# Attention on one Trainium2 core: text queries packed into five tiles per unit, and the turned image probabilities of three heads copied by ScalarE

## The reference, cut to what matters

```
h    = concat(mixer(x), txt)                       # 16 x (128 + 77) x 1024
qkv  = layernorm(h) @ Wqkv                         # 32 query heads of 32, one key head, one value head
s    = q . k * 32**-0.5 + slope[head] * (pos_k - pos_q), masked where pos_k > pos_q
h    = h + (softmax(s) @ v) @ Wo
h    = h + base(layernorm(h)) + routed low-rank part   # 8 experts of rank 16
```

## Time and profile before

| | |
|---|---|
| median of three runs | 1572.31 us |
| profiled execution, its own time | 1572.91 us |
| its span, first to last instruction | 1571.1 us |
| TensorE busy | 1479.0 us (94%) |
| VectorE busy | 1071.4 us (68%) |
| ScalarE busy | 742.8 us (47%) |
| GpSimd busy | 507.4 us (32%) |
| granted TensorE clock, mean | 0.987 |

### The profile page before, as it was taken

How to read it: one execution, slowest core, us unless ns; L and a number is a source line. 1 busy time by engine, 2 the same in 40 slices (tenths; PEclk the granted TensorE clock), 3 DMA queues, 4 the chain that set the end, 5 groups by cost and what they waited for, 6 DMA issues and landing times. The chain is left out here.

```text
span 1571.1 us, 28985 instructions
## 1 busy us (share of the span) xinstructions
PE 1479.0 (94%) x9796; PEld 1311.3 (83%) x9796; DVE 1071.4 (68%) x4158; ACT 742.8 (47%) x2557; POOL 507.4 (32%) x317
## 2 busy tenths in 40 slices
PE   3894999999999999999999989999999999999999
PEld 2784988888888888888887769898989898999898
DVE  7887688888979888897988565353534444444464
ACT  6693586868878786877888431111111111010001
POOL 0001465757475665757544301010101010101010
PEclk9997999999999999999999999999999999999999
DMA  9865754554656364554775251212121212121211
GB/s 307 290 141 123 114 111 87 77 114 66 130 87 120 64 119 83 79 116 71 154 157 113 76 190 47 75 40 80 40 80 40 80 40 80 40 80 40 71 49 41
DMA packets 107646, 153.63 MB, mean 98 GB/s; under 512 B 8948, under 2 KB 93300, under 8 KB 106600
## 3 DMA queue, kind: packets, MB, share of 16 engines
q1 hardware_dynamic: 106712, 151.78, 41.5%
q10 hardware_dynamic: 816, 0.39, 0.1%
HBM read 75.00 MB, written 51.38 MB: 80 GB/s over the span
## 5 line engine op out<-in xcount | busy, mean ns | idle before, releaser
L954 ACT ACTIVATE P<-P,nmax 128x128 f32<-128x128 f32 (+1 forms) x1024 | 434.4, 426 | 91.5 <-DVE nmax L1063 87.4
L1038 POOL TENSOR_TENSOR P<-P,rden 128x512 f32<-128x512 f32 (+1 forms) x256 | 331.9, 1318 | 269.4 <-DVE rden L1069 269.1
L1063 DVE CUSTOM_DVE_ANT_0 P<-sc,mask 128x128 f32<-128x128 f32 (+1 forms) x1024 | 292.7, 323 | 77.2 <-PE sc L829 71.2
L1440 POOL TENSOR_TENSOR ht<-ht 128x1024 f32<-128x1024 f32 (+1 forms) x24 | 58.1, 2422 | 575.5 <-DVE ht L1469 575.5
L859 PE MATMUL pr<-xT_hi,wq_hi 128*128 128x410 f32 x576 | 242.6, 421 | 0.5 <-DVE xT_lo L1090 0.5
L1075 DVE COPY PTR<-pt 128x282 f32<-128x282 f32 x512 | 221.0, 432 | 27.4 <-PE pt L839 26.4
L1337 PE MATMUL b<-w_hi,x2T_hi 128*128 128x390 f32 (+3 forms) x624 | 214.5, 344 | 1.0 <-DVE x2T_lo L1484 1.0
L1337 PE MATMUL b<-w_lo,x2T_hi 128*128 128x390 f32 (+3 forms) x624 | 212.5, 341 | 0.0
L1337 PE MATMUL b<-w_hi,x2T_lo 128*128 128x390 f32 (+3 forms) x624 | 212.0, 340 | 0.0
L859 PE MATMUL pr<-xT_lo,wq_hi 128*128 128x410 f32 x576 | 201.4, 350 | 0.0
L859 PE MATMUL pr<-xT_hi,wq_lo 128*128 128x410 f32 x576 | 200.2, 348 | 0.0
(11 more groups left out here) (212 smaller groups left out, 2931.3 us busy)
## 6 DMA issues: line engine op xcount, KB each, us to landing
Qs<-q_hi SPq DMA_DIRECT2D x128, 205.0 KB, 4.8
ht<-h_dram SPq DMA_DIRECT2D x42, 512.0 KB, 3.7
Qs<-q_lo SPq DMA_DIRECT2D x64, 205.0 KB, 5.7
att_dram<-att SPq DMA_DIRECT2D x64, 205.0 KB, 3.0
at<-att_dram SPq DMA_DIRECT2D x25, 512.0 KB, 4.9
out<-ht SPq DMA_DIRECT2D x23, 512.0 KB, 2.7
h_dram<-Y SPq DMA_DIRECT2D x61, 128.0 KB, 3.2
h_dram<-in_txt SPq DMA_DIRECT2D x1, 4928.0 KB, 40.7
```

The costliest lines, as they stand in the source:

```text
L954: last = nc.scalar.activation(P[rows, j % 2, i, cols], P[rows, j % 2, i, cols], ACT.Exp, scale=-1.0, bias=nmax[at], accum_out=den[at])
L1038: lastp = nc.gpsimd.tensor_tensor(w, w, r, ALU.mult)
L1063: lastv = v.tensor_tensor_reduce(P[0:n, j % 2, i, cols], sc[i % 2][0:n, cols], mask[0:n, m], 1.0, 3.0e38, ALU.add, ALU.min, nmax[0:n, j % ...
L1440: nc.gpsimd.tensor_tensor(rows(t, par)[0:n, :], rows(t, par)[0:n, :], base_b[0:n, :], ALU.add).then_inc(biased, 1)
```

## The change

The eight heads' text queries of a unit (8 x 77 = 616 rows) are copied side by side into a new tile `Qt` and cut into packs of 128, 128, 128, 128 and 104 rows. Steps 0, 2, 3, 5 and 6 make the text scores of one pack each; steps 1, 4 and 7 make image scores alone. The turns follow the same pattern: a turn of head 0, 2, 3, 5 or 6 has the image part of that head and the two parts of a pack, a turn of head 1, 4 or 7 the image part alone. ScalarE makes the copy into `Qt` for the next unit in step 5 (`pack_text`), and also copies the turned image part of heads 1, 4 and 7 (`copy_head`), each after its `exp_head` of that step. VectorE keeps the turns with a pack, now two copies each. The values take three groups of four matmuls in place of two. `turn` waits for two counters, `head_copied` and `pT_copied`, in place of one.

```
+TEXT_ROWS = GH * TXT
+PACKS = [(f, min(128, TEXT_ROWS - f)) for f in range(0, TEXT_ROWS, 128)]
+PACK_STEP = [0, 2, 3, 5, 6]
...
+    Qt = sb("Qt", [128, 2, TEXT_ROWS], F32R)
+    P, Pt = sb("P", [128, 2, GH, CH]), sb("Pt", [128, 2, len(PACKS), S])
+    PTI, PTT = sb("PTI", [128, 2, GH, CH]), sb("PTT", [128, 2, 2, TEXT_ROWS])
+    crow = PTI[:, 1].rearrange("p h t -> p (h t)")[:, 0:16 + 4 * (S + 1)]
...
+    PLAIN = GH - len(PACKS)
+    def packs_upto(i):
+        return sum(at <= i for at in PACK_STEP)
...
             def scores(p, j, i):
                 if i == 0:
...
+                    pe.wait_ge(text_packed, 8 * p + j + 1)
...
+                lasts = nc.tensor.matmul(bank[:, 0:CH], q[:, 0:CH], Ks[0:QR, g // 2, b, 0:CH], start=True, stop=True)
+                k = pack_of(i)
+                if k is not None:
+                    f, n = PACKS[k]
+                    lasts = nc.tensor.matmul(bank[0:n, CH:CH + S + 1], Qt[0:QR, b, f:f + n], Ks[0:QR, g // 2, b, :], start=True, stop=True)
+                lasts.then_inc(scores_done, 1)
...
             def turn(p, j, i):
                 if i % 4 == 0:
                     pe.wait_ge(probs_ready, 16 * p + 2 * j + i // 4 + 1)
-                wait_count(pe, pT_copied, 64 * p + 8 * j + i - 1)
-                bank, src = pt[i % 2], P[:, j % 2, i, :]
-                nc.tensor.transpose(bank[:, 0:CH], src[:, 0:CH], ident[:])
-                nc.tensor.transpose(bank[:, CH:S], src[0:TXT, CH:2 * CH], ident[0:TXT, 0:TXT])
-                nc.tensor.transpose(bank[0:TXT, S:S + TXT], src[0:TXT, 2 * CH:CH + S],
-                                    ident[0:TXT, 0:TXT]).then_inc(transposed, 1)
+                wait_count(pe, head_copied, PLAIN * (8 * p + j) + max(i - 1, 0) - packs_upto(i - 2))
+                wait_count(pe, pT_copied, len(PACKS) * (8 * p + j) + packs_upto(i - 2))
+                bank = pt[i % 2]
+                lastt = nc.tensor.transpose(bank[:, 0:CH], P[:, j % 2, i, :], ident[:])
+                k = pack_of(i)
+                if k is not None:
+                    n, src = PACKS[k][1], Pt[:, j % 2, k, :]
+                    nc.tensor.transpose(bank[:, CH:CH + n], src[0:n, 0:CH], ident[0:n, 0:n])
+                    lastt = nc.tensor.transpose(bank[0:TXT, 2 * CH:2 * CH + n], src[0:n, CH:S], ident[0:n, 0:n])
+                lastt.then_inc(transposed, 1)
...
+            def copy_head(p, j, i):
+                if pack_of(i) is not None:
+                    return
+                act.wait_ge(transposed, 64 * p + 8 * j + i + 1)
+                wait_count(act, av_done, 8 * p + j - 1)
+                nc.scalar.activation(PTI[:, j % 2, i, :], pt[i % 2][:, 0:CH], ACT.Copy).then_inc(head_copied, 1)
...
+            def pack_text(p, j):
+                g, b = j // 2, j % 2
+                for q in q_stacked:
+                    act.wait_ge(q, 16 * STACKS * (4 * p + g + 1))
...
+                wait_count(act, scores_done, 64 * p + 8 * (j - 1))
+                nc.scalar.activation(Qt[0:QR, b].rearrange("p (h t) -> p h t", t=TXT), Qs[0:QR, g % 2, :, b * S + CH:(b + 1) * S].bitcast(F32),
+                                     ACT.Copy).then_inc(text_packed, 1)
...
                         if sj is not None:
                             exp_head(*sj, i)
+                        turning = tj if i >= 4 else aj
+                        if turning is not None:
+                            copy_head(*turning, (i + 4) % GH)
+                        if i == PACK_TEXT_AT and next_unit(p, slot, first, last) is not None:
+                            pack_text(*next_unit(p, slot, first, last))
...
             def copy_turned(p, j, i):
+                if pack_of(i) is None:
+                    return
...
-                v.tensor_copy(PTR[:, j % 2, i, :], pt[i % 2][:, 0:S + TXT]).then_inc(pT_copied, 1)
+                lastc = v.tensor_copy(PTI[:, j % 2, i, :], pt[i % 2][:, 0:CH])
...
+                    lastc = v.tensor_copy(PTT[:, j % 2, :, f:f + n], pt[i % 2][:, CH:3 * CH].rearrange("p (c t) -> p c t", c=2)[:, :, 0:n])
+                lastc.then_inc(pT_copied, 1)
```

More of the change, by code:

```diff
@@ L675, in attention_block @@
     RES_SLOT = [1, 2, 3]
+    PACK_TEXT_AT = 5
     aT = [[w[:, :, r * 128:(r + 1) * 128] for w in xT] for r in range(2)]
@@ L716, in slots, with next_unit, pack_of, columns @@
             yield slot, (MAIN[slot] if last is not None else None), unit(0), unit(1), unit(2)
+    def next_unit(p, slot, first, last):
+        found = att_unit(slot, -1)
+        if found is None or (found[0] and first) or (not found[0] and last is None):
+            return None
+        return p - found[0], found[1]
+    def pack_of(i):
+        return PACK_STEP.index(i) if i in PACK_STEP else None
+    PLAIN = GH - len(PACKS)
+    def packs_upto(i):
+        return sum(at <= i for at in PACK_STEP)
+    def columns(j, i):
+        half, k = i // 4, pack_of(i)
+        return (j % 2, half, slice(i % 4, i % 4 + 1)), None if k is None else (j % 2, half, slice(4 + k - HALF_PACKS[half][0], 5 + k - HALF_PACKS[half][0]))
     with nc.Block() as block:
@@ L951, in exp_head @@
                 act.wait_ge(scores_biased, 64 * p + 8 * j + i + 1)
[L952 to L955, removed]
-                last.then_inc(exp_done, 1)
+                head, pack = columns(j, i)
+                rows = [(CH, P[:, j % 2, i, :], head)]
+                if pack is not None:
+                    rows.append((PACKS[pack_of(i)][1], Pt[:, j % 2, pack_of(i), :], pack))
+                for n, x, at in rows:
+                    at = (slice(0, n),) + at
+                    last = nc.scalar.activation(x[0:n], x[0:n], ACT.Exp, scale=-1.0, bias=nmax[at], accum_out=den[at])
+                last.then_inc(exp_done, 1)
+            def copy_head(p, j, i):
[8 more added lines that the diff above has]
+                    act.wait_ge(q, 16 * STACKS * (4 * p + g + 1))
+                if p + j == 0:
+                    act.wait_ge(rows_ready, 3)
+                wait_count(act, scores_done, 64 * p + 8 * (j - 1))
+                nc.scalar.activation(Qt[0:QR, b].rearrange("p (h t) -> p h t", t=TXT), Qs[0:QR, g % 2, :, b * S + CH:(b + 1) * S].bitcast(F32),
+                                     ACT.Copy).then_inc(text_packed, 1)
             def a_hi(t):
@@ L1034, in body @@
                         pool.wait_ge(recip_done, 16 * q + 2 * j + half + 1)
[L1035 to L1038, removed]
+                        w, r = P[:, j % 2, 4 * half:4 * half + 4, :], rden[:, j % 2, half, 0:4]
+                        nc.gpsimd.tensor_tensor(w, w, r.unsqueeze(2).to_broadcast((CH, 4, CH)), ALU.mult)
+                        packs = HALF_PACKS[half]
+                        w, r = Pt[:, j % 2, packs[0]:packs[-1] + 1, :], rden[:, j % 2, half, 4:4 + len(packs)]
+                        lastp = nc.gpsimd.tensor_tensor(w, w, r.unsqueeze(2).to_broadcast((128, len(packs), S)), ALU.mult)
                         lastp.then_inc(probs_ready, 1)
@@ L1061, in bias_head @@
                 wait_apart(dve, scores_done, 64 * p + 8 * j + i + 1, const_loaded, 32)
[L1062 to L1064 removed]
+                head, pack = columns(j, i)
+                lastv = v.tensor_tensor_reduce(P[:, j % 2, i, :], sc[i % 2][:, 0:CH], mask[:, 0:CH], 1.0, 3.0e38,
+                                               ALU.add, ALU.min, nmax[(slice(0, CH),) + head])
+                if pack is not None:
+                    k = pack_of(i)
+                    n = PACKS[k][1]
+                    lastv = v.tensor_tensor_reduce(Pt[0:n, j % 2, k, :], sc[i % 2][0:n, CH:CH + S], mask[0:n, CH + k * S:CH + (k + 1) * S], 1.0, 3.0e38,
+                                                   ALU.add, ALU.min, nmax[(slice(0, n),) + pack])
                 lastv.then_inc(scores_biased, 1)
@@ L1591, in constants @@
         rows[2 * late:2 * late + 2, 16:] = both.reshape(-1)
-    k, p = np.arange(256)[None, :] - 128, np.arange(128)[:, None]
+    masks = np.zeros((128, MASK_COLS), f)
+    masks[:, 0:CH] = np.where(np.arange(CH)[None, :] > np.arange(CH)[:, None], f(1e30), f(0))
+    for pack, (first, n) in enumerate(PACKS):
+        own = (first + np.arange(n)) % TXT
+        at = CH + pack * S + CH
+        masks[0:n, at:at + TXT] = np.where(np.arange(TXT)[None, :] > own[:, None], f(1e30), f(0))
     steps, coarse = np.zeros((2, 64, HCH, 128), f), np.zeros((2, 64, 2, HCH, AH), f)
@@ L1608, in constants @@
         "ident": np.eye(128, dtype=f),
-        "mask": np.where(k > p, f(1e30), f(0)).astype(f),
+        "mask": masks,
         "rows": rows,
```

39 lines of the change are left out of this document (22 added, 17 removed).

## The result

The changed kernel takes 1603.76 us (median of four runs, 1602.21 to 1604.42) against 1571.73 us of the kernel before on the same chips (1569.68 to 1573.06). The ratio is 1.0204, 95% interval 1.0186 to 1.0221: about 32 us slower. The forecast was 1606 us, with a range of 1560 to 1634.

A forecast was written before the change was run, and what follows sets the result against it. TensorE was taken to bound the attention, VectorE close behind. Terms −3.0+8.4+2.0−2.6 gave +4.8 us a pair, over 7 pairs +33.6 on the profiled 1572.9: 1606 us, range 1560 to 1634.

The forecast's parts named there:

- The new wait: Step 4, six slots: head 0's turn waits 1.4 us for ScalarE's copy of the previous unit's head 7; +8.4 us a pair.
- VectorE's lateness: Two slots with layernorm statistics: VectorE reaches step 3's mask about 1 us late, adding to the wait; 2 us.
- The other copies: Step 2 in seven slots, head 1's copy only in slot 6: TensorE waits for ScalarE's copies; +2.0 us a pair, bounds 0 and 4.
- TensorE's work: Attention: fewer text-score matmuls and transposes, against wider loads and more value matmuls; −0.37 us a unit, −3.0 a pair.
- the sign by which I meant to recognise it: Packed text scores: a wider weight load (0.04 us) would start them later than 0.07 after the image score.
- Older waits: TensorE's existing waits for VectorE, GpSimd and layernorm banks: 6.0 us a pair becomes 3.4, so −2.6, bounds −5 and 0.
- ScalarE behind: Rival: other ScalarE work delays its copies, wait 1.9 us or more, middle +9 a pair; 1625 to 1665 us, chance 0.10.
- The copy in time: Rival: VectorE is the limit, ScalarE's idle time takes the copies, no new waits; −7.3 a pair, 1515 to 1545, chance 0.06.
- Faster, though the wait is there: Rival: wait of 1.0 us replaces most old ones, TensorE saves 0.55 a unit; −2.5 a pair, 1545 to 1569, chance 0.13.
- Packing and ScalarE's idle time as a gain: Second rival, from the skill's advice on emptying PSUM: old copy waits go, none come; 1515 to 1545 us, chance 0.06.
- Waits of the image transposes over 1 us: Sign in the profile: image transposes wait for ScalarE's copy about 48 times by over 1 us, some 60 us in all.
- Put down to ScalarE: Sign: the profile names ScalarE's copy for the transposes' wait; GpSimd or VectorE named there would mean wrong.

The follow-up runs named there:

- loose wait: Changed kernel, but head 0's turn waits only for its own bank's copy (head 6's, two turns old), not the previous unit's head 7: 1546.53 us, ratio 0.9854.
- fourth experiment: Changed kernel with ScalarE's copy ahead of its exponentials and head 0's turn waiting for its own bank's copy only: 1527.68 us, ratio 0.9735.
- VectorE's copies and the tight wait: Changed kernel with VectorE copying heads 1, 4 and 7; head 0's turn still waits for the previous unit's head 7, one turn old: 1562.36 us, ratio 0.9945.
- copy first: Changed kernel with ScalarE's copy put ahead of its exponentials in a step, nothing else: 1540.3 us, ratio 0.9821.

## Why the prediction was right, point by point

**The new wait (+8.4 a pair forecast).** It is there in the six slots named, in step 4, and the loose wait removes it. The chain was 2.17 us by the sum and 2.18 in the row above (412.74 to 414.92), term by term: 0.35 to the mask against 0.30, 0.63 to the first exponential against 0.68, 0.85 for the pair, 0.25 for the copy against 0.30, 0.10 of signalling against 0.05. Over six slots the turn began 9.4 us late a pair by the averages above (against 0.18, and 0.14 in slot 8, where a layernorm chunk precedes). That is the forecast 8.4 plus 1 of the 2.0 that I had put down to VectorE's lateness. Slots 2 and 3, where statistics lie, stand 2.16 and 1.74, against 1.3 in slots 7, 8 and 1 and 1.54 in slot 0.

**The other copies (+2.0).** Against the fourth experiment, where the copy holds nothing up, step 2's turn begins 0.2 to 0.4 us later in slots 1, 2, 3, 5 and 7, 0.04 in slot 0 and no later in slot 8, and head 3's turn in slot 6 begins 0.2 later: 1.8 a pair.

**TensorE's work (−3.0).** It was undersized. The image-only transpose steps last 0.88 us (forecast 0.90), those without text scores 0.95 (0.97), the full ones 1.08 (1.12), and a full step before 1.02, not 1.04. Three, three and two of them make 0.50 us a unit, −4.0 a pair. The values did not grow at all (forecast +0.07 a unit). From the timeline of TensorE after:

```profile
415.84 0.23 PE L858 MATMUL sc<-Ks,Qs 100*128 100x128 f32 x1
415.91 0.31 PE L862 MATMUL sc<-Ks,Qt 100*128 100x206 f32 x1
416.05 0.27 PE L871 MATMUL pt<-ident,P 128*128 128x128 f32 x1
...
416.73 0.22 PE L858 MATMUL sc<-Ks,Qs 100*128 100x128 f32 x1
...
417.90 0.64 PE L888 MATMUL av<-PTI,V 128*32 128x256 f32 x8
...
419.00 0.33 PE L858 MATMUL sc<-Ks,Qs 100*128 100x128 f32 x1
```

The first step takes 0.89; the values 1.10 to the next scores, against 1.09. The packed text score starts 0.07 after the image score, as before, and it was to start later if the wider weight load showed. What differs is the duration (0.31 for 0.27) and the next start, 0.14 later against 0.10. The rows do not tell whether the weight load is the cause of these. So the size of the term (0.04) was right and the sign by which I meant to recognise it was not.

**Older waits (−2.6).** The turns of step 4 and the others had stood about 3.4 us a pair by the same averages, and they no longer stand beside the new ones. The waits at the layernorm banks, which I had left at 1.4, fell to 0.7. From the groups by shape of the changed kernel, one pair (333 to 427 us; busy, mean ns, idle before):

```profile
L916 PEld LDWEIGHTS pr<-ident,ht 128*128 128x128 f32 x16 | 2.3, 141 | 0.7 <-DVE q_lo L1183 0.3 <-DVE xT_lo L1170 0.3
```

Sum: −4.0+9.4+1.8−3.4−0.7 = +3.1, against a period 3.3 us longer and a forecast of +4.8. Three times the error was in the careful direction: too little saved, too much lateness (2.0 for 1.0), too much left at the layernorm banks.

Seven pairs at +4.8 were to make 33.6 us. The profiled executions differ by 30.3, and their parts are others: 19.9 from six pairs at +3.3, 3.0 from the clock in two of these (last section), 5.2 from the seventh interval between copies of V and 4.7 from what follows the last copy, less 2.5 that the changed kernel was ahead at the first copy. So the wait was forecast with its mechanism and nearly its size, but that the total came within 2 us is luck: a lengthening of the period forecast too large by nearly half was offset by the end of the stage and the clock, neither of which I had counted.

**The rivals.** ScalarE behind: no, it waits 18.2 us a pair for VectorE, more than before. The copy in time: no. Faster, though the wait is there: its saving (0.55 us a unit) was nearer than mine, but its wait of 1.0 us was 1.3 or more in every one of the six slots. Packing and ScalarE's idle time as a gain: the Trainium skill, "TensorEngine Tiling (Array Packing)", Performance Considerations, advises both engines for emptying PSUM. Here the copies on ScalarE cost 14 to 41 us after the exponentials, and nothing within 2 us when put first under the loose wait. So in this kernel the sharing alone is no gain; what it costs hangs on where the copy stands and on how old a copy the turn waits for. The Trainium skill, "TensorE: Matmul & The Clock Gate", Part 1, says that ScalarE and VectorE are strictly first in, first out, while TensorE can pull weight loads ahead of matmuls in flight. For ScalarE the traces agree: the copy at 414.57 could have had its input since 413.2, and it follows the exponentials of 413.72 and 414.12.

**Signs.** Waits of the image transposes over 1 us about once a slot: yes. Put down to ScalarE: only in part, and I had written that GpSimd's name there would prove me wrong. It would have misled me without the loose-wait run. The text-score group of 320 instructions: yes. VectorE's busy time 60 us less: yes (61), and GpSimd's too (66). VectorE's waits for scores to grow by some 60 us: no, they went from 68 to 87 us between 199 and 900 us; what grew was its wait for the turns that it copies, from 26 to 77.

## What to carry to other kernels

Check a counting wait at its edges: where `max(i − 1, 0)` replaces `i − 1`, the first of each group waits for one more than it needs, and in a rotation of two buffers that halves the time given to a producer. Here the price came out as the producer's whole chain, queue included, less one step instead of two (2.18 us against 0.86), so work out that chain before moving a copy to an idle engine, and put the copy ahead of what has more time. When a wait on several counters is named after an engine, loosen the counters one by one: the name is only that of the last to finish.

## What the runs showed of the hardware that I had not expected

TensorE's clock fell during the attention. The changed kernel, four stretches from the end of slot 1 to slot 3, then the second and third of them one pair later (start:end, length, busy of each engine, granted clock):

```profile
419.00:423.00 4.00, 3.81 (x30) 3.63 (x27) 3.63 (x16) 3.21 (x13) 0.25 (x1) 1.00 0.66 107
423.00:427.50 4.50, 2.46 (x17) 2.27 (x17) 3.59 (x19) 2.43 (x11) 1.87 (x2) 1.00 1.11 171
427.50:430.90 3.40, 3.40 (x15) 3.17 (x13) 2.77 (x14) 2.22 (x9) 2.06 (x2) 0.51 0.72 88
430.90:434.00 3.10, 3.10 (x39) 2.47 (x38) 1.43 (x7) 1.85 (x6) 0.15 (x1) 0.99 0.05 18
...
517.27:521.77 4.50, 2.46 (x17) 2.27 (x17) 3.60 (x19) 2.44 (x11) 1.87 (x2) 1.00 1.11 172
521.77:525.17 3.40, 3.40 (x41) 2.70 (x40) 2.59 (x14) 2.39 (x10) 2.21 (x2) 1.00 0.68 82
```

After 4.5 us in which TensorE was busy for only 2.46, with one wait of 2 us in them, the granted clock stood at 0.51, the level of 1.2 GHz, for 3.4 us, and then at 2.4 GHz again. The step in it lasted 1.56 us:

```profile
427.49 0.25 PE L858 MATMUL sc<-Ks,Qs 100*128 100x128 f32 x1
...
429.05 0.31 PE L858 MATMUL sc<-Ks,Qs 100*128 100x128 f32 x1
```

It happened in two of the pairs, which lasted 94.3 and 94.2 us against 92.7, so there the wait cost 1.5 us beyond itself. One pair later the same stretch, with the same 2.46 us of TensorE's work, was followed by the full clock, so these rows do not tell what decides. The kernel before shows no such stretch between 153 and 841 us. In the profiled runs of the experiments it came in five pairs with VectorE's copies and the tight wait (periods of 88.8 to 88.9 us against 87.3), in six with the packing at step 7, in three and in one of the unpacked kernels with the tight wait (ScalarE's and VectorE's copies), and, before the last slots of the stage, in none with the loose wait and none with copy first. So a part of what the tight wait costs comes by way of the clock: about 8 us in that profiled run with VectorE's copies, 3 us in the changed kernel.

The other is ScalarE's 128x128 copy: 257 ns, a quarter of a microsecond, below the 0.30 that I had drawn from longer ones.
